# Attention step: at each place the transposed scores go ahead of the scores for the maximum

## The reference

```python
Q = Q * cos + _rotate_half(Q) * sin          # B=2, S=1024, nh=16, d=32
K = K * cos + _rotate_half(K) * sin
scores = jnp.einsum('bhqd,bhkd->bhqk', Q, K) / scale
scores = jnp.where(causal, scores, jnp.float32(-jnp.inf))
attn = jax.nn.softmax(scores, axis=-1)
out = jnp.einsum('bhqk,bhkd->bhqd', attn, V)
...
hdn = jax.nn.silu(g) * u
out = jnp.einsum('ti,hi->th', hdn, down_w) * down_s
```

## Time and profile before

| what | value |
|---|---|
| time, median of 3 runs | 753.57 us (751.13 to 759.17) |
| the profiled execution: its time, its span | 756.7 us, 754.9 us |
| granted PE clock, mean | 0.995 of full speed |
| PE busy | 732.0 us, 97% of the span |
| PEld, DVE, ACT, POOL busy | 537.5, 442.2, 308.7, 246.4 us |

### The profile page before, as it was taken

How to read it: one execution, slowest core, us unless ns; L and a number is a source line. 1 busy time by engine, 2 the same in 40 slices (tenths; PEclk the granted TensorE clock), 3 DMA queues, 4 the chain that set the end, 5 groups by cost and what they waited for, 6 DMA issues and landing times.

```text
span 754.9 us, 10665 instructions
## 1 busy us (share of the span) xinstructions
PE 732.0 (97%) x3563; PEld 537.5 (71%) x3563; DVE 442.2 (59%) x1103; ACT 308.7 (41%) x641; POOL 246.4 (33%) x224
## 2 busy tenths in 40 slices
PE   7999999979999999999999999999999999999996
PEld 7788888755665655555555547878788888888884
DVE  6979584987777777777777637863243125114113
ACT  3232232256666666666655562223322232222221
POOL 0626251502114142414141436832232223223222
PEclk9999999999999999999999999999999999999998
DMA  8586568635566666666676475650001001001001
GB/s 281 187 280 232 197 251 278 251 127 158 167 168 180 166 177 181 170 180 175 167 194 167 111 208 171 250 227 1 0 3 55 0 1 56 0 0 56 1 1 58
DMA packets 54318, 104.39 MB, mean 138 GB/s; under 512 B 14820, under 2 KB 18404, under 8 KB 53748
## 3 DMA queue, kind: packets, MB, share of 16 engines
q1 hardware_dynamic: 54264, 103.72, 44.7%
HBM read 69.62 MB, written 38.21 MB: 143 GB/s over the span
## 4 chain that ended last, share of the span: by engine, by line
PE 83%; issue 5%; DVE 4%; DMA 3%; ACT 2%; POOL 2%; SPq 0%; DVEq 0%; POOLq 0%; ACTq 0%
PE ps L1101 38%; PE ps L1240 17%; PE ps L1316 9%; PE ps L1219 8%; PE ps L1126 8%; DMA q_st<-neg_max_T 2%; PE ps L1093 2%; POOL hid_lo L592 1%; ACT p L680 1%; ACT o_raw L687 1%; PE ps L1137 1%; PE ps L1160 1%; SPq L421 0%; DMA x_st<-in_x 0%; DVE stats L796 0%
## 5 line engine op out<-in xcount | busy, mean ns | idle before, releaser
L680 ACT ACTIVATE p<-ps 128x384 f32<-128x384 f32 (+3 forms) x384 | 159.5, 489 | 35.0 <-PE ps L1219 34.4
L841 DVE CUSTOM_DVE_ANT_0 masked<-ps,mask_qk 128x512 bf16<-128x512 f32 (+1 forms) x240 | 113.6, 502 | 66.9 <-PE ps L1126 66.0
L1219 PE MATMUL ps<-q_st,k_st 99*128 99x384 f32 (+2 forms) x384 | 135.6, 361 | 4.2 <-ACT p L680 1.3
L1240 PE MATMUL ps<-p,v_slot 128*64 128x512 f32 (+3 forms) x768 | 137.3, 494 | 0.2 <-ACT o_raw L687 0.2
L1052 DVE SCALAR_TENSOR_TENSOR hid<-ps,us_sb,silu 128x512 f32<-128x512 f32 x44 | 33.0, 751 | 165.2 <-PE ps L1101 159.5
L1126 PE MATMUL ps<-k_st,q_st 96*128 96x512 f32 (+2 forms) x384 | 127.8, 355 | 1.0 <-DVE row_max L841 0.9
L592 POOL TENSOR_TENSOR hid_lo<-hid,hid_hi 128x512 fp32r<-128x512 f32 x44 | 56.8, 1292 | 172.2 <-ACT hid_hi L756 172.2
L561 POOL TENSOR_SCALAR_AFFINE_SELECT p<-p 128x512 f32<-128x512 f32 x64 | 40.7, 637 | 202.9 <-ACT p L680 202.8
L1240 PEld LDWEIGHTS ps<-p,v_slot 128*64 128x64 f32 x768 | 50.1, 136 | 74.3 <-issue 62.0
L1126 PEld LDWEIGHTS ps<-k_st,q_st 96*128 96x128 f32 x384 | 72.5, 190 | 26.4 <-issue 17.7
L1219 PEld LDWEIGHTS ps<-q_st,k_st 99*128 99x128 f32 x384 | 72.3, 190 | 18.7 <-ACT p L680 9.6
(11 more groups left out here) (119 smaller groups left out, 1081.9 us busy)
## 6 DMA issues: line engine op xcount, KB each, us to landing
qk_scratch<-st_hi SPq DMA_DIRECT2D x32, 512.0 KB, 3.8
q_st<-qk_scratch SPq DMA_DIRECT2D x32, 384.0 KB, 3.9
k_st<-qk_scratch SPq DMA_DIRECT2D x32, 384.0 KB, 5.0
flag_st<-in_ffn SPq DMA_DIRECT2D x32, 264.0 KB, 2.8
ffn_copy<-in_ffn SPq DMA_DIRECT2D x32, 264.0 KB, 3.2
qk_scratch<-st_lo SPq DMA_DIRECT2D x16, 512.0 KB, 3.8
o_T<-o_raw SPq DMA_DIRECT2D x32, 128.0 KB, 4.6
rec_l<-rec_rows SPq DMA_DIRECT2D x32, 128.0 KB, 3.3
```

Source lines behind the costliest of these rows:

```text
L680: act.activation(p32[:, at:at + q0 + w - keep], ps[:, ST_BANK + i % ST_RING, keep - q0:w], ACT.Exp, scale=SCALE).then_inc(exp_done, 1)
L841: ins = dve.tensor_tensor_reduce((masked_a if u < 2 else masked)[:, s_before(i) % 2, col:col + kept], scores, mask_qk[:, 512 - kept:512], ...
L1219: pe.matmul(ps[:, ST_BANK + i % ST_RING, 0:w], k_st[0:K_ALL, slot, kt * P:(kt + 1) * P], q_st[0:K_ALL, slot, q0:q0 + w], start=True, stop= ...
L1240: ins = pe.matmul(ps[VW * a:VW * (a + 1), o_bank(u, half), q0 - 512 * half:512], v_slot[:, slot, kt, :], p32[:, at:at + n], start=(kt == 0 ...
```

## The change

Within a place the two calls change order: `shifted_piece(t, i)` comes first, then `score_bank(t + 2, i)`. The transposition of the maxima at place 4 stays where it is, behind the PV group of place 3 and ahead of ST4. The waits go along with their calls; none is added or taken away.

```diff
                 for i in range(NPC):
                     if i == M_ENTRY and t < HEADS - 1:
                         transpose_max(t + 1)
-                    elif i != M_ENTRY and t + 2 < HEADS:
-                        score_bank(t + 2, i)
                     if t < HEADS:
                         shifted_piece(t, i)
+                    if i != M_ENTRY and t + 2 < HEADS:
+                        score_bank(t + 2, i)
                     if t >= 2 and i in PV_AFTER[t % 2]:
                         output_products(...)
```

## The result

The changed kernel takes 758.75 us in the median (757.26 to 763.86), the one before 755.31 us (751.13 to 759.17), 19 runs each: ratio 1.0061 with a 95% interval of 1.0045 to 1.0078. That is 0.6% slower, 4.6 us, with 3.4 to 5.9 as its interval; +6.3 us, 0.8%, was forecast, a little above it. The profiled execution took 761.5 us with a span of 759.8 us, against 754.9.

What follows compares the result with a forecast made beforehand. PE's work was taken to bound attention, with ACT setting ST's place with little or no slack. Terms 2.5 + 2.4 + 1.7 - 0.3 + 0 = +6.3 us on the median 753.6 gave 759.9 us; range 752.5 to 764.

Steps and rivals of the forecast that it cites:

- The rule for a held ST: ST waiting for ACT acts as if started 0.15 us after its exponential's end, or at its turn, whichever is later.
- A: Even steps, places 4 to 9: S7 runs after ST7's wait instead of inside it; 14 x 0.18 = 2.5 us.
- B: Odd steps, places 4 to 9: without S7 ahead, ST7 and ST8 come late on exponentials; 14 x 0.17 = 2.4 us.
- C: Odd step's second PV group to the next PV: ST1 and ST3 held by exponentials; 13 x 0.13 = 1.7 us.
- D: Five ST0 waiting for the maxima's DMA, S0 now behind them: between +0.3 and -0.9 us, taken as -0.3.
- E: Steps 0 and 1, without PV: T's later S and filled waits cancel; taken as 0, bounds -0.2 and +0.4 us.
- R2: Rival: S between ST3 and PV covers waits for ACT, ST7's waits go too; 744.9 us, over 1% faster; chance 0.05.
- R3: Rival: a whole 512-column S uncovered in 41 stretches; +9.8 us, 763.4; chance 0.24 including whatever else exceeds +7.5.
- R1: Rival: ACT runs ahead earlier, B and C vanish, A shrinks; nothing measurable or slightly better, 752.5 to 755.0 us; chance 0.15.
- The slack on DVE's side: Cover between the negated maximum's last step and T: 1.10 us becomes about 0.86, so later S costs nothing.
- S waiting for DVE in a full step: Sign that the prediction is wrong; the S ring was claimed not to bind in full steps.
- The table of waits: PE's waits: ST's holds by ACT were to grow from 16 to over 40, their sum from 6.3 to about 12 us.

Runs made afterwards that it cites:

- mid: Kernel before with ST ahead of S at places 5 to 9 only, S first elsewhere: ratio 1.0054 to the kernel before.
- ends: Kernel before with ST ahead of S at places 10, 11 and 0 to 3 only, S first elsewhere: ratio 1.0020.
- late6: Pair with ACT's first output copy of even steps moved behind exponential 6: ratio to the kernel before 0.9963 with S first, 1.0004 with ST first.
- extra: Pair with one tiny activation added on ACT behind odd steps' second output copy: 759.3 us in the changed kernel, 755.4 in the one before, one execution each.
- late6_s: Kernel before (S first) with ACT's first output copy of even steps moved behind exponential 6: ratio 0.9963.
- rec_s: Kernel before (S first) with SP's load of the reciprocals moved behind the next maxima: ratio 1.0042.
- rec_st: Changed kernel (ST first) with SP's load of the reciprocals moved behind the next maxima: ratio 1.0107 to the kernel before.
- rec2_st: Changed kernel (ST first) with the reciprocals' load behind the maxima and POOL's scaling behind the masks: ratio 1.0088 to the kernel before.
- rec2_s: Kernel before (S first) with the reciprocals' load behind the maxima and POOL's scaling behind the masks: ratio 0.9994.
- best_s: Kernel before (S first) with reciprocals' load behind the maxima, POOL's scaling behind the masks, ACT's first even-step output copy behind exponential 6: 747.58 us, ratio 0.9913.

## Why the prediction was right, and where not

**The mechanism was right**: the S of its own place left the wait of a held ST. mid and ends put the loss at places 5 to 9, late6 shows that its size in even steps follows ACT's hold, extra shows an ST held in one order and not in the other by the same end of an exponential. The rule for a held ST fits as well: in the changed odd step exponential 4 ends at 261.32, and the matmul behind ST7 starts as if ST7 had started at 261.48. The trace's 5.4 us stand nearer to the forecast than the terms deserve: 0.5 of them are the two waits of S9, which no term had and which differ from execution to execution.

**A, +0.18 in even steps:** measured 0.18 (2.41 to 2.59), 2.5 us as forecast. ST7 stayed at T + 1.48.

**B, +0.17 in odd steps:** measured 0.125, 1.75 us and not 2.4. ST7 and ST8 did what the rule said. The term was mis-sized mainly because I left exponential 5's end where it was. ST5 comes one S sooner now, and the pair of exponentials 4 and 5 takes 0.87 us in place of 0.90, so ST8 is freed at T + 1.36 and no longer at T + 1.39. Exponential 5 by itself, before and now, in ACT's timelines:

```profile
259.27 0.49 ACT L680 ACTIVATE p<-ps 128x384 f32<-128x384 f32 x1
```

```profile
261.22 0.48 ACT L680 ACTIVATE p<-ps 128x384 f32<-128x384 f32 x1
```

Before, it started 0.04 behind the recorded end of ST5 (258.89 + 0.34 = 259.23), just as exponential 4 did behind ST4's (258.82 and 258.86), in each of the odd steps; now it starts 0.25 behind it. So ST5 had released it. The rest of the 0.045 is that the old order already lost about 0.03 from ST7 to PV (0.84 us, the pace gives 0.81), where I counted 0.01.

**C, +0.13 behind the odd step's second PV group:** measured 0.02, 0.3 us and not 1.7. The step that failed is the sentence that exponential 10 ends at the same time whether ST10 came first or second. In the trace before, ST10 ran to 262.70 + 0.39 = 263.09 and exponential 10 began at 263.12, 0.53 behind the start of the output copy; now it begins 0.48 behind it (264.70 and 265.18), since ST10 has ended 0.10 before. So it was ST10 and not the copy that released it, by 0.05. The extra pair bears this out: there the added activation keeps ACT busy beyond ST10's end, and exponential 10 starts 0.57 behind the copy in both orders. With exponential 0 gaining 0.11 as well (its end 2.19 behind the first matmul of the stretch before, 2.08 now), ST1 and ST3 are at their turns. The rows for this were there: an end of ST10 at 263.09 beside a start at 263.12 is a release. Two rows of PE and ACT from before that say so:

```profile
262.70 0.39 PE L1219 MATMUL ps<-q_st,k_st 99*128 99x512 f32 x1
```

```profile
262.59 0.59 ACT L687 COPY o_raw<-ps 128x512 f32<-128x512 f32 x1 [1.63 <-PE ps L1240]
```

**D, -0.3:** measured +0.1 in one trace, and no measured number is worth much here. How late the maxima land in every fourth step differs widely, 4.1 to 6.4 us after T in the two traces, and 7.3 once in late6_s, against 3.1 to 3.8 elsewhere. rec_s shows that the reciprocals' load ahead is what makes it so. Neither of my two bounds, landing fixed to T or to the heads' loads, describes it.

**E, 0:** the two T of steps 0 and 1 moved by 0.2 and back by 0.1, as weighed.

**The rivals.** R2 falls with ends. R3, a whole S of 512 columns in all 41 stretches, falls with B and C. Of R1 the part came true that ACT gains from an earlier ST (B and C), which is why A, B and C give 4.6 us and not 6.6. The slack on DVE's side held for T. But the prediction named S waiting for DVE in a full step as a sign that it is wrong, and S9 does so in step 12 for 0.45 us and in step 20 for 0.09: 0.5 us that no term had, with a cause that it did not think of (the last section).

**The table of waits** was forecast with more than 40 holds and about 12 us and shows 29 and 11.0: C's are missing.

**The clock** was not 9 tenths in every slice, as the prediction reads the earlier trace rows: the last slice has 8. It lies behind the attention stage, so no term hangs on it.

## What to carry to other kernels

Where two streams of matmuls alternate in one queue and one of them is held now and then, put the free one ahead: at the held place it fills the wait; at the places with slack the order was worth 0.03 us or less here. Price it as the overlap of the free instruction with the wait, and ask for each engine in the ring which end released its next instruction, since an order that hurts one side may release the other sooner. A wait that looks like the cost may be better taken at its source: here ACT's copy in the wrong place cost 4.3 us by the rows, about as much as the order, and moving one engine's work gave a gain only when what stood behind it in the next queue moved too.

## What the runs showed that was not expected

**An instruction of DVE of 0.70 us lasts 2.4 to 2.9 us beside one of POOL.** Timelines of DVE, then POOL, of the changed kernel:

```profile
269.04 2.69 DVE L954 SCALAR_TENSOR_TENSOR flag_bits<-flag_st,flag_bits 128x528 int32<-128x528 int32 x1
271.65 0.68 DVE L841 CUSTOM_DVE_ANT_0 masked<-ps,mask_qk 128x512 bf16<-128x512 f32 x1
```

```profile
268.79 2.37 POOL L550 TENSOR_TENSOR o_T<-o_T,rec_l 128x1024 f32<-128x1024 f32 x1 [1.57 <-DMA rec_l<-rec_rows]
```

The test of the weights (L954) reads two operands from SBUF and begins 0.25 us behind POOL's product, which reads two as well; it ends 0.57 after that one ends at 271.16. S5's maximum waits behind it, and S9 on PE for that one's bank, 0.45 us, the step 12 of the changed kernel. In the kernel before, POOL's product begins at 267.57, after the test, and all 32 tests take 0.69 to 0.71. Where in the changed kernel the test begins 0.10 us ahead of the product (306.74 and 306.84), the test keeps its 0.70 and the product lasts 2.84 in place of 2.37. The long test came twice in the changed kernel, once in mid, twice in rec_st, three times in rec2_st (0.97 to 1.17 us of PE each), once in rec2_s (1.18), never in best_s. The Trainium skill ("SBUF — State Buffer", section "SBUF: two separate sides") says that the pair of ports that DVE and GpSimd share is locked for the whole instruction, on DVE's side by an operation with two SBUF inputs against a GpSimd one that reads SBUF, and that whichever starts second blocks; these rows agree. So part of the spread of these kernels hangs on whether the DMA of the reciprocals lets POOL's product begin just ahead of the test or just behind it. That an order which brings S later has less cover for it is not shown: rec2_s, with S first, lost as much to one such test as rec2_st.
